# Transformer tower, expert stages: two of the four hidden blocks get their rounded part from VectorE instead of a second activation

## The reference, cut to what matters

```python
# layer 0: the two experts chosen for a sequence, for all of its tokens
h = gelu(einsum('bsd,edh->ebsh', x, w1) + b1)      # 128 -> 512
eo = gelu(einsum('ebsh,eho->ebso', h, w2) + b2)    # 512 -> 128
out = einsum('ebso,be->bso', eo, g)
...
# layer 1: two experts chosen for each token
for e in range(8):
    hdn = gelu(flat @ W1[e] + b1[e])
    y = hdn @ W2[e] + b2[e]
    out = out + gates[:, e:e + 1] * y
```

## Time and profile before

| | |
|---|---|
| median of 3 runs | 1641.43 us (1638.7 to 1645.34) |
| profiled execution, its own time | 1635.83 us |
| span of the profiled execution | 1634.0 us |
| PE busy | 1281.6 us (78%) |
| DVE busy | 1030.9 us (63%) |
| ACT busy | 1016.2 us (62%) |
| POOL busy | 526.5 us (32%) |
| mean granted clock of PE | 0.873 of full speed |

### The profile page before, as it was taken

The page is one execution under the profiler, slowest core; times in us unless marked ns, Lnnn a source line. Parts: engine busy times, 40 slices in busy tenths (PEclk is TensorE's granted clock), DMA queues, the critical chain, the costliest instruction groups (busy, mean ns, idle before and its releaser), DMA issues. The chain is left out here.

```text
span 1634.0 us, 31526 instructions
## 1 busy us (share of the span) xinstructions
PE 1281.6 (78%) x9689; PEld 843.2 (52%) x9689; DVE 1030.9 (63%) x2828; ACT 1016.2 (62%) x1358; POOL 526.5 (32%) x453
## 2 busy tenths in 40 slices
PE   3699998999998999369999948667762299999950
PEld 2344444444444444147777736556552177777740
DVE  5255756566666653437888757666653389899944
ACT  0487777787788789218888834323320188888840
POOL 3212222222221211200000011555544347667665
PEclk8699999999999999779999968667765599999985
DMA  3451606061615240011111000000010445555519
GB/s 90 80 116 21 123 13 130 19 119 27 112 38 96 55 78 2 9 35 45 39 39 46 7 11 1 30 33 31 33 34 26 143 136 147 143 152 156 147 47 308
DMA packets 134467, 118.99 MB, mean 73 GB/s; under 512 B 30459, under 2 KB 112310, under 8 KB 134350
## 3 DMA queue, kind: packets, MB, share of 16 engines
q1 hardware_dynamic: 114798, 93.75, 25.0%
q0 software_dynamic: 9216, 16.94, 3.1%
q10 hardware_dynamic: 10336, 6.82, 1.8%
HBM read 76.63 MB, written 42.37 MB: 73 GB/s over the span
## 5 line engine op out<-in xcount | busy, mean ns | idle before, releaser
L343 ACT ACTIVATE a_probs<-a_psS 128x1024 f32<-128x1024 f32 x512 | 491.1, 1031 | 123.3 <-PE a_psS L426 96.9
L438 PE MATMUL a_psO<-a_probs,a_v 128*32 128x256 f32 x4096 | 281.8, 394 | 24.7 <-DVE a_o_sb L643 24.1
L807 ACT ACTIVATE f_g_hi<-f_psH,f_b_hid 128x512 fp32r<-128x512 f32 x288 | 200.6, 697 | 55.4 <-PE f_psH L71 47.5
L922 DVE TENSOR_TENSOR f_g_lo<-f_g,f_g_hi 128x512 fp32r<-128x512 f32 x288 | 197.7, 688 | 53.3 <-ACT f_g L809 51.2
L1738 POOL DMA_INDIRECT result<-f_out,f_idx x160 | 186.5, 1166 | 114.8 <-issue 57.6
L426 PE MATMUL a_psS<-a_qs,a_ks 50*128 50x512 f32 x1024 | 193.1, 456 | 25.1 <-issue 12.4
L809 ACT ACTIVATE f_g<-f_psH,f_b_hid 128x512 f32<-128x512 f32 x288 | 199.7, 694 | 0.0
L438 PEld LDWEIGHTS a_psO<-a_probs,a_v 128*32 128x32 f32 x4096 | 108.5, 111 | 169.5 <-issue 88.5
L1164 POOL DMA_INDIRECT queue<-all_row,all_idx x128 | 127.0, 992 | 102.8 <-DVEq L1554 47.2
L1249 POOL TENSOR_TENSOR a_rs<-a_veps,all_half 128x8 f32<-128x8 f32 x16 | 26.6, 1662 | 337.5 <-DVE a_veps L83 337.4
L426 PEld LDWEIGHTS a_psS<-a_qs,a_ks 50*128 50x128 f32 x1024 | 78.9, 190 | 97.8 <-ACT a_probs L343 47.3
(11 more groups left out here) (289 smaller groups left out, 2235.1 us busy)
## 6 DMA issues: line engine op xcount, KB each, us to landing
f_raw<-W SPq DMA_DIRECT2D x80, 256.0 KB
a_qs<-qparts SPq DMA_DIRECT2D x96, 128.0 KB, 4.6
a_ks<-kparts SPq DMA_DIRECT2D x84, 128.0 KB, 4.5
f_rows<-queue SPq DMA_DIRECT2D x40, 260.0 KB, 2.6
qparts<-a_parts SPq DMA_DIRECT2D x16, 512.0 KB, 2.6
f_raw<-w SPq DMA_DIRECT2D x32, 256.0 KB, 2.6
kparts<-a_parts SPq DMA_DIRECT2D x14, 512.0 KB, 3.3
out_y<-result SPq DMA_DIRECT2D x8, 512.0 KB, 11.4
```

Source lines behind the costliest of these rows:

```text
L343: nc.scalar.activation(probs[u % NPR][:, :], psS[score_buffer(u)][:, :, :].rearrange("p a n -> p (a n)"), ACT.Exp).then_inc(exp_done, 1)
L438: last = nc.tensor.matmul(psO[32 * g:32 * g + 32, a * HALF:(a + 1) * HALF], v[par][:, 2 * hp + p, kt, :], probs[u % NPR][:, cols:cols + HA ...
L807: nc.scalar.activation(g_hi[i][:, n, :], psH[n][:, :], ACT.Gelu, bias=b_hid[i][:, n:n + 1])
L922: nc.vector.tensor_tensor(g_lo[i][:, n, :], g[:, n, :], g_hi[i][:, n, :].bitcast(F32), ALU.subtract).then_inc(lo_done, 1)
```

## The change

For blocks 1 and 3 of the hidden layer ScalarE's first activation (L807) is dropped. Once `g` is there, VectorE copies it into `g_hi`, rounding as it writes, drains, and subtracts as before. Blocks 0 and 2 stay. The change holds for both expert stages.

```diff
--- before.py
+++ after.py
@@ -804,7 +804,8 @@
                 act.wait_ge(h_ps, m * NB + (n + 1))
                 if n == 0:
                     act.wait_ge(y_ps, m + 1)
-                nc.scalar.activation(g_hi[i][:, n, :], psH[n][:, :], ACT.Gelu, bias=b_hid[i][:, n:n + 1])
+                if n % 2 == 0:
+                    nc.scalar.activation(g_hi[i][:, n, :], psH[n][:, :], ACT.Gelu, bias=b_hid[i][:, n:n + 1])
                 act.wait_ge(lo_done, m * NB + (n + 1))
                 nc.scalar.activation(g[:, n, :], psH[n][:, :], ACT.Gelu, bias=b_hid[i][:, n:n + 1]).then_inc(g_done, 1)
                 if n == 0 and then is not None:
@@ -919,6 +920,9 @@
 
             m, i = it * R + k, k % 2
             dve.wait_ge(g_done, m * NB + (n + 1 + NB))
+            if n % 2:
+                nc.vector.tensor_copy(g_hi[i][:, n, :], g[:, n, :])
+                dve.drain()
             nc.vector.tensor_tensor(g_lo[i][:, n, :], g[:, n, :], g_hi[i][:, n, :].bitcast(F32), ALU.subtract).then_inc(lo_done, 1)
```

## The result

The changed kernel takes 1681.09 us in the median of four runs (1679.5 to 1683.99), the kernel before 1641.14: a ratio of 1.0233, 95% interval 1.021 to 1.0256, 40 us slower. The forecast was 1675 in a range of 1658 to 1692. The profiled execution has a span of 1677.7 us against 1634.0.

The account below looks back on a forecast made before the run. TensorE was taken as the bound, with VectorE becoming the token stage's bound after the change. Token stage +30 and sequence stage +4 us on the 1641.4 us median gave 1675 us, 2.1% slower; range 1658 to 1692.

Parts of the forecast that it names:

- The relief of ScalarE: Both stages: two activations fewer, 1.2 us an item; ScalarE is not the bound, only earlier `g` by 0.59 us could help.
- The copy at 0.50 us: VectorE, blocks 1 and 3: each rounding copy with its drain costs 0.50 us, 1.00 us an item; bounds 0.35 and 0.61.
- The estimate of 0.33 us: VectorE's copy by the skill's 58 + 512/2 cycles at 0.96 GHz; the token stage would lose 17 us instead of 30.
- VectorE's serial time at 6.58 us: Token stage: VectorE's own need per item of 6.80 us, leaving 0.22 us slack; 7.58 us with the copies.
- What held the item at 6.80 us: Token stage: TensorE taken as the bound, own need 6.4 us an item plus 0.4 us waits; VectorE's slack 0.22 us.
- waits that stay: Rival, token stage: VectorE still waits 0.2 to 0.4 us an item for `g` or rows; 1684 to 1692 us; chance 0.09.
- Sum of the token stage: Token stage: 1.00 - 0.22 = 0.78 us an item lost over 39 bodies, 30.4 us; with the prologue's 0.5 back, +30.
- 39 bodies: Token stage: VectorE's bodies with `low` in them, each taken to lose 0.78 us, 30.4 us together.
- The sequence stage: Second-layer weight split ends 0.58 us later, TensorE waits 1.2 instead of 0.64 us once a round, 8 rounds: +4 us.
- The clock's fall: Rival, token stage: TensorE's 1.2 us waits per item lower its granted clock; 1688, up to 1710 us; chance 0.10.
- Cheaper copies: Rival: the copy costs 0.35 to 0.42 us and the sequence stage nothing; 1660 to 1665 us; chance 0.13.
- Not slower: Rival: VectorE's idle time is all waiting that earlier `g` dissolves, copies at most 0.33 us; 1636 us; chance 0.05.

Follow-up runs that it names:

- the runs with one stage: Changed kernel with the change in only one expert stage, the other as before: ratio 1.0027 for the sequence stage, 1.0215 for the token stage.
- the copies alone: Kernel before plus VectorE's copy and drain for blocks 1 and 3 into an unread tile, ScalarE keeping both activations: ratio 1.0296.
- the relief alone: Changed kernel without VectorE's copies; blocks 1 and 3 use the rounded part of the block before, so values differ: ratio 0.9987.
- the rows early: Kernel before, token stage: SP loads a later chunk's rows ahead of its wait for the second-layer weight split: ratio 0.9967.
- the swapped splits: VectorE's second-layer weight split and chunk low part change places: ratio 1.0329 on the changed kernel; 1.018 on the kernel before with rows loaded early.
- the results sent by SP: Changed kernel, token stage: one plain SP transfer an item replaces GpSimd's four indirect ones, output in item order: ratio 1.0083.

## Why the prediction was right, point by point

**Direction, mechanism and size.** +40 us measured, +34 forecast. VectorE becomes the bound of the token stage, the sequence stage pays through the late split, the clock stays. All three were in the prediction, and the runs with one stage, with the copies alone and with the relief alone bear them out.

**The relief of ScalarE is worth nothing where VectorE is the bound.** Right for the token stage (293.6 us without, 294.4 with it). In the sequence stage it is worth 5.8 us.

**The copy at 0.50 us.** Right for block 1 (0.49) and for both blocks in the sequence stage (0.50 and 0.49). Wrong for block 3 in the token stage, where it is 0.65: the term was mis-sized by 0.15 us in 25 of 28 bodies. The trace of before has weight copies of 0.52 us too (last section), 3 in 64, so the longer kind was there to be seen. The estimate of 0.33 us, from the Trainium skill's figure ("VectorE: DVE Perf Modes", section on the TRN2 errata), is lower than any copy here: 0.41 to 0.60 us. That section says itself that the figure comes out short and puts the fixed part at about 150 cycles instead of 58. By that, an estimate, the copy takes (150 + 256) / 0.96 = 423 ns, and the 0.42 us of the rows agree.

**VectorE's serial time at 6.58 us.** It is 6.65 (the item with the rows early). The earlier trace rows had it: a body of 6.92 us with a round's branch, which is 0.37 us shorter without, makes (6.92 + 3 x 6.55) / 4 = 6.64. With 0.50 + 0.65 for the copies the item is 7.80; the changed kernel has 7.77.

**What held the item at 6.80 us.** This is the one step of the mechanism that failed. The prediction calls TensorE the bound, and takes VectorE's waits for `g` as the slack that the earlier `g` gives back. The slack was 6.80 - 6.65 = 0.15 us, and an earlier `g` alone gave none of it back (6.83 with the relief). The loop over the split, SP's queue and the rows held the item, and with it TensorE, whose 0.4 us of waits an item had no owner in the prediction. The rival "waits that stay" names this very loop, but only for the kernel after. For this change it made no difference: with 7.8 us an item VectorE waited 0.8 us in 260. That the forecast did not suffer from it is in part luck; for what to do next it matters.

**Sum of the token stage.** 30.4 us forecast, 33.6 to 35.8 measured, so 3 to 5 too little. Two terms were too small, the copy of block 3 by 0.15 and the serial time by 0.07 us an item. One was too large: 39 bodies are counted, but the last two of the stage are short in all kernels (4.9 and 2.1 us). Over the 37 others the corrected terms make (0.78 + 0.22) x 37 = 37.0 us, against 35.8 measured.

**The sequence stage.** +4 forecast, +3.2 measured. Block 1 as the payer and block 3 as nearly free were both right. The wait grew by 0.37 us instead of 0.58.

**The rivals.** The clock's fall did not come: 1.00 and 0.99, though TensorE could not use some 1.4 us (7.77 - 6.4) of every item. Cheaper copies and waits that stay did not come either. "Not slower" needed copies of at most 0.33 us; the cheapest of the changed kernel took 0.42, and 0.49 with its drain. The wait of the transposes for `f_x_lo` in the token stage, 24.1 us by the weight loads, stood in no part of the prediction; it cost nothing more, since VectorE sets the item.

## What to carry to other kernels

Before moving work from one engine to another, compare serial times and not busy shares: VectorE looked idle for 10% of the token stage and had 0.15 us of 6.80 to give.

Check by an experiment what holds the item where it is, for instance by taking the relief alone. When that gains nothing, the cause of the waits is elsewhere, here a load that stood behind an unrelated wait in SP's queue. Moving it ahead gave 5.9 us of stage and a ratio of 0.9967 (0.995 to 0.9983); no run of this study that does the whole computation has a better one.

A wait that is seen ending last is no proof that its owner may be moved past others, as the swapped splits show.

## What the runs showed of the hardware that was not expected

A rounding copy of 128x512 on VectorE is lengthened by an indirect transfer of GpSimd that ends while it runs, and by how much depends on the place of the end. In the changed kernel (1340 to 1560 us) a transfer ends 0.18 or 0.19 us into a weight copy, 25 times, and the copy takes 0.43 to 0.44 us; it ends 0.33 to 0.34 us into a copy of L924, 26 times, and the copy takes 0.58 to 0.59. In the changed kernel with the splits swapped it ends 0.26 or 0.27 us into a weight copy 26 times, and the copy takes 0.52 or 0.53. In each of these cases the copy goes on for some 0.25 us behind the transfer's end. Since the periods are fixed, the same copy meets the same end in body after body.

The other way round, a transfer is lengthened by what VectorE has just started, and more by a subtraction than by a copy. In the kernel before (same stretch) 52 of 128 transfers take 1.37 to 1.49 us instead of 0.98. Each of them starts behind the start of an L922, whose two inputs lie in SBUF. The 7 that start just behind an L902, one of whose inputs lies in PSUM, all take 0.98, and 8 that start just behind a weight copy take 1.21 to 1.25. One meeting of each kind in the kernel before, a copy of 0.52 us and a transfer of 1.47:

```profile
1403.83 0.98 POOL L1738 DMA_INDIRECT result<-f_out,f_idx  x1 [0.72 <-issue]
1404.55 0.52 DVE L62 CAST f_w_hi<-f_raw 128x512 fp32r<-128x512 f32 x1
...
1412.25 0.69 DVE L922 TENSOR_TENSOR f_g_lo<-f_g,f_g_hi 128x512 fp32r<-128x512 f32 x1
1412.32 1.47 POOL L1738 DMA_INDIRECT result<-f_out,f_idx  x1 [0.30 <-issue]
```

The long transfers do not bound either kernel, as GpSimd still waits for VectorE's results (19.1 us between 1340 and 1560 us before, 83.6 between 1340 and 1600 after). The long copies cost the changed kernel 0.16 us in nearly every item. The counts show where the meetings fall; what inside the engines makes one wait for the other was not tested.

GpSimd's indirect transfers also run on behind the stage. In the kernel before, the last one starts 12 us after the last group of `turn_y`:

```profile
1587.85 0.98 POOL L1738 DMA_INDIRECT result<-f_out,f_idx  x1 [0.30 <-issue]
```

From that group (1575.79) to the end of the span, 58.2 us go by; with the results sent by SP it is 1655.4 - 1611.1 = 44.3 us. The last stage's loads of the results wait for the transfers: the first one starts 18.6 us after that group (1594.39) in the kernel before, and 4.3 us after it with the results sent by SP. These 14 us, not the copies, are the larger part of what that run gained over the changed kernel, whose own tail is 58.7 us. Whether the rows can leave sooner at their proper places was not tried.
